# The order of routing, normalization and weight splits while the shared layer of a mixture of experts starts

## The reference, cut to what matters

```python
x = x + layernorm(attention(layernorm(x)))
xt = layernorm(x).reshape(2048, 512)
probs = softmax(xt @ Wg)                     # 8 experts
eidx = argmax(probs); gate = probs[eidx]
oh = one_hot(eidx)
pos = (cumsum(oh, axis=0) * oh).sum(-1) - 1  # place within the expert
keep = pos < 256
xd[eidx * 256 + pos] = xt                    # rows beyond 256 are dropped
h = silu(xd @ W1) * (xd @ W3); oe = h @ W2   # per expert, 704 hidden
out = oe[...] * gate * keep
shared = silu(xt @ sw1) * (xt @ sw3) @ sw2   # all tokens
x = x + layernorm(out + shared)
```

## Time and profile before

| | us |
|---|---|
| median of 3 runs | 808.99 |
| lowest and highest | 807.75, 809.15 |
| the profiled execution, its own time | 810.11 |
| span of the profiled execution | 808.4 |
| TensorE busy | 773.3 (96%) |
| VectorE busy | 562.5 (70%) |
| ScalarE busy | 420.8 (52%) |
| GpSimd busy | 145.4 (18%) |

### The profile page before, as it was taken

How to read it: one execution, slowest core, us unless ns; L and a number is a source line. 1 busy time by engine, 2 the same in 40 slices (tenths; PEclk the granted TensorE clock), 3 DMA queues, 4 the chain that set the end, 5 groups by cost and what they waited for, 6 DMA issues and landing times. The chain is left out here.

```text
span 808.4 us, 13818 instructions
## 1 busy us (share of the span) xinstructions
PE 773.3 (96%) x5077; PEld 650.2 (80%) x5077; DVE 562.5 (70%) x1200; ACT 420.8 (52%) x840; POOL 145.4 (18%) x229
## 2 busy tenths in 40 slices
PE   6999999999999999999999998999999999999994
PEld 4787787777777777787878886999999999887884
DVE  5764898578897567777588445566676666758676
ACT  5464352445656566677354343666676666633120
POOL 3300010510101213233254422000000000013122
PEclk9999999999999999999999999999999999999998
DMA  7789565976766798862259432586778786546444
GB/s 233 227 273 349 187 181 177 271 221 175 217 183 183 179 255 244 236 179 82 94 194 337 185 132 70 179 261 211 211 206 265 207 263 208 170 152 200 139 157 144
DMA packets 117636, 162.39 MB, mean 201 GB/s; under 512 B 17380, under 2 KB 65508, under 8 KB 117568
## 3 DMA queue, kind: packets, MB, share of 16 engines
q1 hardware_dynamic: 113984, 153.54, 62.7%
q0 software_dynamic: 3584, 7.97, 3.3%
HBM read 107.24 MB, written 55.05 MB: 201 GB/s over the span
## 5 line engine op out<-in xcount | busy, mean ns | idle before, releaser
L1576 ACT ACTIVATE PT<-bank 128x512 f32<-128x512 f32 x128 | 74.2, 596 | 54.7 <-PE bank L1216 50.5
L1216 PE MATMUL wide<-W2H,HH 128*128 128x512 f32 x308 | 100.7, 392 | 0.5 <-ACT OUTR L1501 0.5
L1984 DVE TENSOR_TENSOR SIL<-bank,SIL 128x256 f32<-128x256 f32 (+1 forms) x72 | 36.8, 512 | 70.9 <-ACT SIL L1661 70.5
L1661 ACT ACTIVATE SIL<-bank 128x256 f32<-128x256 f32 (+1 forms) x72 | 32.6, 453 | 100.4 <-PE bank L1216 95.3
L1216 PE MATMUL bank<-XT,W13H 128*128 128x256 f32 (+1 forms) x336 | 76.6, 322 | 0.0
L1501 ACT ACTIVATE HH<-SIL 128x256 fp32r<-128x256 f32 (+1 forms) x72 | 35.2, 489 | 64.8 <-DVE SIL L1984 64.8
L1216 PEld LDWEIGHTS wide<-W2H,HH 128*128 128x128 f32 x308 | 57.8, 188 | 13.0 <-ACT OUTR L1501 1.3
L1216 PE MATMUL wide<-W2L,HH 128*128 128x512 f32 x168 | 65.8, 391 | 0.4 <-DVE W2L L1895 0.4
L1986 DVE TENSOR_TENSOR HH<-SIL,HH 128x256 fp32r<-128x256 f32 (+1 forms) x72 | 37.0, 514 | 39.9 <-ACT HH L1501 38.5
L1216 PEld LDWEIGHTS bank<-XT,W13H 128*128 128x128 f32 x336 | 55.0, 188 | 4.7
L1216 PE MATMUL bank<-WQL,W13H 128*128 128x256 f32 (+1 forms) x168 | 55.5, 330 | 0.0
(11 more groups left out here) (303 smaller groups left out, 2066.2 us busy)
## 6 DMA issues: line engine op xcount, KB each, us to landing
R<-in_L_ffn_W_dram SPq DMA_DIRECT2D x48, 512.0 KB, 5.3
scr_q<-hl SPq DMA_DIRECT2D x16, 512.0 KB, 3.7
scr_k<-hl SPq DMA_DIRECT2D x16, 512.0 KB, 4.0
R<-in_L_ffn_sw_dram SPq DMA_DIRECT2D x12, 512.0 KB, 5.0
QSe<-scr_q SPq DMA_DIRECT2D x36, 128.0 KB
KSe<-scr_k SPq DMA_DIRECT2D x36, 128.0 KB
R<-_attn_hidden_states_dram SPq DMA_DIRECT2D x16, 256.0 KB, 3.7
scr_qtok<-H2A SPq DMA_DIRECT2D x16, 256.0 KB, 3.7
```

Of the source, the lines that this page charges most:

```text
L1216: return pe.matmul(ps, a, b, start=start, stop=stop, skip_group_check=True)
L1576: sc.activation(pt.buf[:, :], hold["s", n, u].buf[:, :], ACT.Exp, scale=SCALE).then_inc(*a_exp.up(n, u))
L1661: sc.activation(sil.buf[r, 0:N], a_in, ACT.Silu).then_inc(*a_inner.up("silu", q, m))
L1984: dv.tensor_tensor(sil[r, 0:N], b_in, sil[r, 0:N], ALU.mult).then_inc(*d_inner.up("mul", q, m))
```

## The change

It has two parts, both in the written list. In `work` the count of four tiles no longer stands directly behind the logits of the fourth tile but behind the `h_turn` of the next one in the same call. Since the counts that meet a `h_turn` of VectorE are that of tiles 0 to 3 (n = 8), VectorE there makes the low half of tile 4 first. In `ffn_pass` the call of `work` moves up: from behind the loads and splits of the column to directly behind `up` (and `prepare`, which does nothing in passes 0 and 1).

```diff
@@ work @@
                         do(name, t)
-                        if name == "h_logits" and t % 4 == 3:
-                            do("route_count", t // 4)
+                    if name == "h_turn" and 0 <= n - 5 < 16 and (n - 5) % 4 == 3:
+                        do("route_count", (n - 5) // 4)
@@ ffn_pass @@
                     do("up", q, m)
                     if q >= 2:
                         prepare(q + 1, m)
+                    if q == 1 or q == 0 and m < 5:
+                        work()
                     for j, g3 in reload.pop((q, m), []):
                         do("load_13", j, g3, 0)
                         do("load_13", j, g3, 1)
@@
                                 do("load_13", 1, g3, 0)
                                 do("load_13", 1, g3, 1)
-                    if q == 1 or q == 0 and m < 5:
-                        work()
```

## The result

The changed kernel takes 812.67 us (median of 11 runs, 809.99 to 815.79), the kernel before 809.97 (11 runs, 806.82 to 813.05, the three behind the 808.99 of the prediction among them): ratio 1.0047, interval 1.0027 to 1.0066. It is slower by 0.3 to 0.7%. In a second session the ratio was 1.0018, interval 0.9992 to 1.0043, which does not exclude no change. The profiled execution took 812.67 us around a span of 810.9.

A forecast was written before the change was run, and what follows sets the result against it. TensorE, 96% busy, bounds the kernel, so only its waits or low clock matter. The middle of -1.46 (no drop or absorbed) and 0 (drop returns), -0.73, gave 810.11 - 0.73 - 1.12 = 808.3 us; range 806.6 to 810.2.

The forecast's parts named there:

- the first term of the part on VectorE: Pass 0, step m=0: W2L starts at 402.45 and W13L for column 2 at 403.05, 0.60 us later.
- The second new wait: Pass 0, before column 3: TensorE waits 1.56 us for W13L, behind the step with the placing.
- The clock: Open term in pass 0: a half-clock drop after the second new wait costs 1.55 us at most, after the first nothing.
- the -0.86: Pass 0: column 5 starts at 426.18 instead of 427.04, 0.86 us earlier, of which the half clock is 1.55.
- another -1.12: Whole kernel: step from the profiled execution's 810.11 us to the median of the runs, 808.99, 1.12 lower.
- the first new wait: Pass 0, before column 2: TensorE waits 1.43 us for W13L, so column 2 starts 0.31 later than before.
- The end of pass 1: Last placing moves 1.33 us earlier, so TensorE's wait for the expert's rows goes: 0.60 us gained, bounds 0 and 0.60.
- rival (c): End of pass 1 gives nothing because the rows' load waits for something else than the placing: 808.9 us, chance 0.12.
- ScalarE's copies and normalization: Pass 0: three split copies behind the next tile's normalization cost nothing; at most one 0.7 us wait per step otherwise.
- The six loads: SyncE's loads of the next weights, issued from 422.07, go 4 to 5 us later, hidden: cost zero.
- (a): Rival: VectorE's four steps each wait 0.70 us at the tile's subtraction for ScalarE's copy: +2.1, 811.1 us, chance 0.12.
- (b): Rival: both old waits and the half clock go, splits never late: -4.4, 804.6 us (or 806.8), chance 0.10.

The follow-up runs named there:

- small_after: Changed kernel with GpSimd adding only 16 of 512 columns of each tile to the residual: 812.89 us against 812.76, ratio 0.9991.
- memset_after: Changed kernel with GpSimd's residual addition replaced by one fill of the tile: 812.61 us against 812.43, ratio 0.9983.
- place_first: Kernel before with only the last placing of pass 1 moved ahead of the splits: 812.20 us against 812.43, ratio 0.9994.
- step_only: Kernel before with only the token step moved ahead of the splits, the count left in place: 816.01 us, ratio 1.0034.
- pass1: Changed kernel with the token step ahead of the splits in pass 1 only, behind them in pass 0: 814.42 us, ratio 1.0028.
- pass0: Changed kernel with the token step ahead of the splits in pass 0 only, behind them in pass 1: 814.21 us against 811.03, ratio 1.0042.
- count_only: Kernel before with only the count moved, the token step left behind the splits: 812.92 us against 812.76, ratio 1.0003.
- late_store: Kernel before with the stores of pass 1's first two output tiles behind the loads of the expert's first rows: 807.20 us against 806.91, one execution.
- spread: Kernel before with the count behind the next tile's bias and pass 0's W2L made at columns 3, 4 and 5: 815.91 us against 811.03, ratio 1.0052.

## Why the prediction was wrong

The forecast was 808.3 us and no measurable change; the measured 812.67 lies outside the range, and the change is slower. About 1.0 of the 4.4 us between the two is the base: the median of the kernel before is 809.97 over 11 runs, 808.99 over the three of the prediction. The rest is the change.

**The step that failed** is the first term of the part on VectorE: "W2L at 402.45, W13L for column 2 at 403.05". The order, the waits and the place of each operation came as worked out, the duration did not. Start to start, the four W2L took 1.19, 0.60, 1.51 and 1.20 instead of 0.60 each: 2.10 more, and all of it reached TensorE. Columns 2 to 5 are 0.71, 0.73, 1.72 and 2.31 later than forecast, 0.16 of it from the later start of the stretch. Without the lengthening (small_after) A was 35.02, and the forecast's own figures give 34.99 (426.18 + 429.91 - 427.04 - 394.06), with a wait of 1.33 + 0.16 = 1.49 where 1.43 was forecast. The second new wait, forecast at 1.56, shows where the clock stays full: 1.03 + 0.16 = 1.19 in memset_after, 0.37 less, of which 0.28 is the placing without an addition beside it. The sum over the order was right.

A smaller slip: the step of column 4 in pass 0 was said to have nothing between, but the fifth part of W2 is split there; that W2L (435.22) now meets an addition too, outside of A, and no wait followed.

The sentence on GpSimd, "GpSimd gets its inputs earlier and keeps its order", asked of GpSimd only when it is served, not what it does to its neighbour. In the old order the step's last VectorE operations were followed by the product from PSUM and a wait; in the new one by two or three subtractions with both operands in SBUF.

The rule was to be had. The Trainium skill (SBUF — State Buffer, Who interferes with whom) states that a VectorE instruction with two SBUF inputs contends with a GpSimd instruction that reads SBUF, and not with one that only writes it. By that rule the W2L behind the moments meets the addition, and the traces agree on each side: 1.27 beside the addition, 0.68 beside a fill, 0.68 for the product with one operand in PSUM. The section calls the shared port pair an exclusive lock, and that agrees too: W2L ends 0.55 after the addition, nearly its own 0.60 from start to start, as if it had only begun there.

**The clock.** A term was counted on the wrong base, the second step that failed. The half clock of the earlier trace rows was booked as 1.55 of gain inside the -0.86, and then the profiled run was scaled to the median by another -1.12. But the old order has it absorbed in four of its six traces with one whole addition. Against such an execution the new order was to be +0.4 (34.99 against 34.59), not -0.86. That a stretch at half clock behind the first new wait costs nothing was right.

**The end of pass 1.** Forecast -0.60 with zero as the other bound; no gain shows. B is 77.14, 77.65, 77.66, 77.56 and 77.14 with the placing early (changed kernel twice, place_first, step_only, pass1), mean 77.43, and 77.42, 77.52, 77.31 with it late (before, pass0, count_only), mean 77.42, with up to 0.5 between traces of one kind. This is the mechanism of rival (c), that the load waits for something else, and late_store shows the store of the shared tiles as a part of that.

**What held.** ScalarE's copies and normalization cost nothing: W2H ended at 401.61, ahead of W2L's start at 402.62. The six loads were issued from 428.57, 6.5 later than before where 4 to 5 was forecast, and ScalarE, which reads them first, did not wait for them (467.51, WQH from R, behind its own normalization).

**The rivals.** (a), VectorE's steps grow, had the sign, and at 811.1 about three quarters of the size (2.1 of 2.7), but named ScalarE's copy as the cause and the tile's subtraction as the place; that one kept 0.68. Its sum was worked from the same wrong base. (b) did not occur: the splits were late.

**The sum in hindsight**, against an execution of before with its half clock absorbed: +0.4 for the order, +2.1 for the lengthened subtractions, 0 at the end of pass 1, together +2.5 us. The changed kernel's A + B (114.29 and 114.76 against 112.0) gives +2.3 and +2.8; the medians differ by 2.70 and 0.93. Against an execution like the profiled one, whose half clock costs 1.26, the same sum gives +1.2, and the traces +1.0 and +1.5. That the timed runs mix the two kinds in the ratio of the traces is not shown.

## What to carry to other kernels

When an operation is moved, look up what every other engine does in its new place, not only who waits for whom: two engines that never wait for each other can still share a way to memory, and a VectorE instruction with two SBUF operands beside a reading GpSimd instruction waits for nearly all that is left of it (0.59 to 0.91 us here, of 0.71 to 1.03 left). Look for it in the trace before the change: the same operation with two durations is the sign. Take the old length of a stretch from more than one execution before a clock dip in it is booked as a gain. A length that ends at a marker is only comparable if no work has moved across the marker.

## What the runs showed of the hardware

- A held-up subtraction ends 0.55 to 0.56 us after the addition, whether W2L or the hidden one, and GpSimd's next small power grows from 0.54 to 0.99 when it meets the subtraction in turn.
- GpSimd's indirect scatters take 1.50 instead of 0.97 beside two-operand subtractions of VectorE: one in the kernel before (subtractions until 497.14), two in the changed one (until 498.48). The first scatter of these four lies beside them as well and keeps 0.97, so it is not one to one, and no run tests it. That it costs time at the end was not shown.
- The mean granted clock of an execution of the kernel before lies between 0.984 and 0.995. What that leaves of the span, (1 - clock) x span, is 4 to 13 us. In three sessions (35, 29 and 35 executions) the times had standard deviations of 2.8, 2.1 and 2.5 us, and 1.8, 1.6 and 1.5 once this part was taken off: about half of the variance between executions goes with the clock. Whether as cause or as effect (in spread the clock fell behind a wait of 3.25) is not shown.
